# Four graph layers on one core: degree sums two tiles later, the joint share of the row sums added by VectorE, x written by ScalarE, fifth sweep's residual by blocks

## The chip, the cores and the metric

One core of a Trainium2 chip. The metric is the device time of one execution in microseconds; the median of three runs is given, and the profile is of one further execution.

## What is computed

Four graph layers over the same dense 4096 x 4096 matrix `adj` and 4096 x 128 features `x`, each followed by a residual and a layer norm over the 128 features. In short:

```python
# layer 0
inv_deg = 1.0 / (sum(adj, axis=1) + beta)
x = layernorm(x + inv_deg[:, None] * (adj @ x + beta[:, None] * x) @ kernel + bias)
# layer 1
h = x
for W, b in ((W1, b1), (W2, b2), (W3, b3)):       # widths 20, 20, 128
    h = relu(adj @ (h @ W) + b)
x = layernorm(x + relu(h + x))
# layer 2
d = 1.0 / (sqrt(sum(adj, axis=1)) + 1e-8)
x = layernorm(x + d[:, None] * (adj @ (d[:, None] * (x @ W + b))))
# layer 3
S = (x @ W_l) @ (x @ W_r).T
x = layernorm(x + adj @ x + gamma * (softmax(S) @ x) @ W_h @ W_g)
```

## The kernel before

**Stages.** The matrix is read six times (sweeps 0 to 5), then comes the attention part. Sweep 0 is layer 0, sweeps 1 to 3 are the three products of layer 1 (narrow: 20 columns), sweep 4 is layer 2 and sweep 5 is `adj @ x` of layer 3. A sweep has eight rows c (512 nodes each), and a row has 16 half tiles n of 128 x 1024 (512 KB). TensorE accumulates a row in one PSUM bank.

**Split tiles.** A product in full float32 takes TensorE four passes. Where it pays, a tile is split: ScalarE rounds it into t_hi (float32r), VectorE subtracts into t_lo, and TensorE does three single-pass products for each 512 columns, six per tile: t_hi with x_hi and x_lo (L1452, L1453), then t_lo with x_hi (L1456). Both t_hi and t_lo are rings of four, so ScalarE can't start tile u before TensorE has finished tile u-4. In sweep 0 the tiles that are split are, row by row: none; 1, 5, 8, 12, 14, 15; 1, 3, 4, 5, 8, 10, 12, 14, 15; 1, 3, 4, 5, 7, 8, 9, 11, 13, 14, 15; 0, 2, 3, 4, 6 to 11, 13 to 15; all but 4; all; all. The rest are plain (L1460). In sweeps 4 and 5 all tiles are split (L872, L1173, L1607, L1608, L1612).

**Joint tiles.** In sweep 0, tiles whose h is known already are used at once for sweep 1 as well (the joint product, L1469, into another bank, every second tile). With them TensorE also gets their share of the row sums of `adj`, which ScalarE stores in `sums[:, c]` (L749). The tiles that aren't joint (16, 14, 12, 10, 8, 6, 4 and 2 of the rows 0 to 7) are summed by VectorE: `row_sum` into rsum (L986, L990), then `fold` into row_folded (L997).

**The epilogue of a row** runs inside the next row, at places fixed by the tile number n. In sweep 0, for row c-1 inside row c:
- TensorE, after tile 1: `epilogue_1`: e0 (four products with k0, L1349), then e1: for each of four blocks a one-column product of row_folded (L1353) and one of sums with the row picker (L1356; rows 1 to 7 only). After tile 9 the transpose of xn, after tile 11 the product with w1.
- ScalarE: after its tile 2 `evacuate` and `store_ahead`; after tile 4 `second` (square root of the degree sum in e1, L754); after 8 `deviation`; after 10 `normalise` (L774, into xn); after 12 `transposed`.
- VectorE: after tile 4 `residual_1` (degrees, then e0 times inv, L1072), after 5 `residual_2` (plus xb, L1095), after 6 `statistics`, after 8 `scales`; `fold` right after the last tile that isn't joint (tile 15, 13, 13, 13, 13, 11, 7, 1 of the rows 0 to 7).
- GpSimd: xb (L632), then bx (L653), and when xn is there the copy of xn into x (L658).

Each engine works its own list in order, so whatever stands behind a waiting instruction waits too. In sweep 4 the order is alike (all tiles split; `residual_1` L1082 and `residual_2` L1095 at tiles 4 and 5 on VectorE), and GpSimd does stationary5_lo (L639), xb (L635) and the copy into x (L674) for each row. Sweep 5 needs x as st5_hi and st5_lo.

Of the kernel before, what the change touches and what calls it, by code (L numbers as in the profile page):

```python
# [15 lines left out]
P = 128  # L16
# [34 lines left out]
    "xb": (0, 3, 4, 5), "bx": (0,), "xw": (0, 3, 4), "at": range(6), "sq": (0,),  # L51
    "h1": (1, 2), "dinv0": (0,), "deg": (0,), "inv": (0,), "dg2": (0,), "t1": (0, 3, 4),
    "resid": (0, 3, 4), "b3": (3,), "lb": (3,), "bst": (0, 3, 4), "agg": (0, 3, 4), "var": (0, 3, 4), "std": (0, 3, 4),
    "rc": (0, 3, 4), "rstd": (0, 3, 4), "norm": (0, 3, 4), "xt": (0, 3), "ht": (5,), "uw": (0, 1, 2),
    "vw": (3,), "xfin": (5,), "mm1": range(6), "rr": (0,), "mm2": (1, 2), "tx": (0, 3), "mu": (0, 3),
}

# [134 lines left out]
def build(nc, adj_s, x_dram, beta_in, ident_in, comb_in, w, out):  # L192
    with ExitStack() as ctx:
# [46 lines left out]
        with ExitStack() as swp:  # L240
# [26 lines left out]
            xn = sb("xn", [P, CW], F32, swp)  # L267
# [343 lines left out]
        def _(pool):  # L611
# [3 lines left out]
            def keep_old_x(s, c):  # L615

                if s == 5:
                    if first(c):
                        pool.wait_ge(S["resid"], done("resid", 4, NC - 1))
# [3 lines left out]
                    pool.wait_ge(S["xw"], done("xw", 4, NC - 1))  # L623
# [12 lines left out]

            def stationary5_lo(d):
                pool.wait_ge(st5_hi_done, d + 1)
                nc.gpsimd.tensor_tensor(cols(st5_lo, d), cols(x, d), cols(st5_hi, d).bitcast(F32),  # L639
                                        ALU.subtract).then_inc(st5_lo_done, 1)  # L640

            def first_row(c):
                for n in range(NG):
# [11 lines left out]
                    if n == 13 and c > 0:  # L655
                        pool.wait_ge(S["norm"], done("norm", 0, c - 1))
                        alone(pool)
                        nc.gpsimd.tensor_copy(cols(x, c - 1), xn[:, :]).then_inc(S["xw"], 1)  # L658

            def step(s, c, par):  # L660
# [4 lines left out]
                if s == S4 and not (isinstance(c, int) and c < 2):  # L665
                    stationary5_lo(c - 2)
                if s == S5 and first(c):
                    stationary5_lo(NC - 2)
                if ps in STAGES["xb"]:
                    keep_old_x(ps, pc)  # L670
                if ps in STAGES["xw"]:
                    pool.wait_ge(S["norm"], done("norm", ps, pc))
                    alone(pool)
                    nc.gpsimd.tensor_copy(cols(x, row(ps, pc)), xn[:, :]).then_inc(S["xw"], 1)  # L674
                if s == S5 and first(c):
                    stationary5_lo(NC - 1)
# [294 lines left out]
        def _(dve):  # L971
# [785 lines left out]
```

## Time and profile before

| what | us |
|---|---|
| median of 3 runs (1320.33 to 1321.06) | 1320.92 |
| profiled execution | 1323.62 |
| its span, first to last instruction | 1321.8 |
| TensorE busy (share of the span) | 1266.1 (96%) |
| VectorE busy | 969.1 (73%) |
| ScalarE busy | 800.6 (61%) |
| GpSimd busy | 268.5 (20%) |

The rest of the profile is read by stretch: a row of sweep 0 lasts 31 to 39 us, a row of sweeps 4 and 5 22 to 23 us. "Idle before" in a timeline, in square brackets, is how long the engine stood still before that instruction and what ended it. L numbers are lines of the kernel.

### The profile page before, as it was taken

Reading aid. Unit: us, or ns where it says so; the run is one execution under the profiler, and the core shown is the slowest. Engines: PE = TensorE matmul, PEld = TensorE weight load, DVE = VectorE, ACT = ScalarE, POOL = GpSimd, SP = SyncE. Lnnn points to the kernel's source line nnn. Section 1 sums busy time; section 2 is a strip of 40 time slices with the busy share of each in tenths; the row PEclk is TensorE's granted clock in tenths of the full one; section 3 lists DMA queues with packets and bytes.
Section 4 is the critical chain, followed back from the end, with each engine's and each line's share of the span. In section 5 each row is a group of like instructions: output and inputs, shape, how many; then the busy total and the mean of one; then the engine's idle time right before and its main releaser. Section 6 shows DMA issues by size and latency. Waiting matters only on the chain.

```text
span 1321.8 us, 17914 instructions
## 1 busy us (share of the span) xinstructions
PE 1266.1 (96%) x6139; PEld 831.9 (63%) x6139; DVE 969.1 (73%) x1242; ACT 800.6 (61%) x966; POOL 268.5 (20%) x175
## 2 busy tenths in 40 slices
PE   8999999989999899999999999998999999999987
PEld 3566666643332334787877888886676777767764
DVE  7998987620000556999999898877888888778885
ACT  1334556511110224787878777766978787788795
POOL 0211111000000110021112000005333343354355
PEclk9999999889999899999999999999999999999998
DMA  9978766589999699899999999960000000000000
GB/s 366 321 260 311 264 253 248 176 327 346 365 346 409 249 384 383 303 375 356 363 374 345 363 357 386 359 249 0 1 0 0 1 0 1 1 18 14 1 1 32
DMA packets 82817, 294.34 MB, mean 223 GB/s; under 512 B 9658, under 2 KB 11322, under 8 KB 82746
## 3 DMA queue, kind: packets, MB, share of 16 engines
q1 hardware_dynamic: 80496, 292.59, 59.2%
q10 hardware_dynamic: 2250, 0.82, 0.2%
q8 instruction: 43, 0.70, 0.2%
q14 instruction: 28, 0.23, 0.1%
HBM read 291.27 MB, written 2.10 MB: 222 GB/s over the span
## 4 chain that ended last, share of the span: by engine, by line
PE 69%; DVE 12%; ACT 6%; issue 6%; DMA 5%; POOL 1%; DVEq 0%; POOLq 0%; ACTq 0%; SPq 0%
PE acc L1546 8%; PE acc L1612 6%; PE acc L1607 6%; PE acc L1608 6%; PE acc L1694 5%; DMA raw<-in_adj_s 5%; PE acc L1460 4%; PE acc L1452 3%; PE acc L1456 3%; PE acc L1453 3%; DVE peak L1225 3%; DVE t_lo L1173 2%; ACT ring L927 2%; PE rs L1469 2%; PE rs L1551 2%
## 5 line engine op out<-in xcount | busy, mean ns | idle before, releaser
L1173 DVE TENSOR_TENSOR t_lo<-raw,t_hi 128x1024 fp32r<-128x1024 f32 x256 | 311.0, 1259 | 26.6 <-ACT t_hi L872 21.8
L872 ACT ACTIVATE t_hi<-raw 128x1024 fp32r<-128x1024 f32 x256 | 261.6, 1055 | 40.5 <-PE acc L1612 39.5
L1607 PE MATMUL acc<-t_hi,st_hi 128*128 128x512 f32 x512 | 201.9, 394 | 0.8 <-ACT t_hi L872 0.8
L704 POOL TENSOR_TENSOR ring_lo<-ring,p_hi 128x1024 fp32r<-128x1024 f32 x64 | 155.5, 2429 | 219.4 <-ACT p_hi L921 219.3
L1608 PE MATMUL acc<-t_hi,st_lo 128*128 128x512 f32 x512 | 199.5, 390 | 0.0
L1612 PE MATMUL acc<-t_lo,st_hi 128*128 128x512 f32 x512 | 159.5, 393 | 5.8 <-DVE t_lo L1173 5.1
L1247 DVE TENSOR_TENSOR ring<-ring,e 128x1024 f32<-128x1024 f32 x128 | 153.9, 1210 | 0.1
L915 ACT ACTIVATE ring<-ring 128x1024 f32<-128x1024 f32 x128 | 134.2, 1054 | 26.0 <-DVE ring L1247 25.8
L1694 PE MATMUL acc<-ring,x 128*128 128x512 f32 x256 | 120.4, 592 | 0.0
L1612 PEld LDWEIGHTS acc<-t_lo,st_hi 128*128 128x128 f32 x512 | 95.0, 188 | 30.6 <-DVE t_lo L1173 11.4
L1607 PEld LDWEIGHTS acc<-t_hi,st_hi 128*128 128x128 f32 x512 | 96.1, 188 | 21.8 <-DVE st_lo L1033 1.2
L1608 PEld LDWEIGHTS acc<-t_hi,st_lo 128*128 128x128 f32 x512 | 96.2, 188 | 19.8 <-issue 0.2
L1008 DVE TENSOR_TENSOR t_lo<-raw,t_hi 128x1024 fp32r<-128x1024 f32 x72 | 91.4, 1296 | 17.5 <-ACT t_hi L808 17.5
L808 ACT ACTIVATE t_hi<-raw 128x1024 fp32r<-128x1024 f32 x72 | 74.3, 1054 | 37.4 <-PE acc L1456 24.9
L1225 DVE TENSOR_TENSOR peak<-e,peak 128x1024 f32<-128x1024 f32 x54 | 66.1, 1223 | 40.9 <-ACT ring L927 40.8
L1225 DVE TENSOR_TENSOR peak<-rs,peak 128x1024 f32<-128x1024 f32 x61 | 74.5, 1221 | 24.5 <-ACT ring L927 24.0
L674 POOL COPY x<-xn 128x512 f32<-128x512 f32 (+1 forms) x17 | 13.3, 785 | 361.4 <-ACT xn L774 361.4
L1048 DVE TENSOR_TENSOR at<-acc,sums 128x512 f32<-128x512 f32 x19 | 13.1, 689 | 98.8 <-PE acc L1546 84.7
L927 ACT ACTIVATE ring<-rs 128x1024 f32<-128x1024 f32 x62 | 63.3, 1021 | 36.6 <-PE rs L1651 36.1
L1546 PE MATMUL acc<-raw,h_a 128*20 128x512 f32 x384 | 82.7, 601 | 2.5 <-DMA raw<-in_adj_s 1.5
L1460 PE MATMUL acc<-raw,x 128*128 128x512 f32 x160 | 74.6, 610 | 6.5 <-DMA raw<-in_adj_s 6.5
L1452 PE MATMUL acc<-t_hi,x_hi 128*128 128x512 f32 x172 | 77.5, 451 | 0.0
(231 smaller groups left out, 2240.1 us busy)
## 6 DMA issues: line engine op xcount, KB each, us to landing
raw<-in_adj_s SPq DMA_DIRECT2D x518, 512.0 KB, 5.7
kept_t<-in_adj_s SPq DMA_DIRECT2D x8, 512.0 KB, 7.2
x<-in_x SPq DMA_DIRECT2D x4, 512.0 KB, 8.9
kept_l<-in_adj_s SPq DMA_DIRECT2D x4, 512.0 KB, 7.5
kept_s<-in_adj_s SPq DMA_DIRECT2D x4, 512.0 KB, 6.6
kept_v<-in_adj_s SPq DMA_DIRECT2D x4, 512.0 KB, 6.6
kept_e<-in_adj_s SPq DMA_DIRECT2D x4, 512.0 KB, 8.6
kept_late<-in_adj_s SPq DMA_DIRECT2D x4, 512.0 KB, 11.4
```

What stands on the lines that cost most here:

```text
L704: nc.gpsimd.tensor_tensor(ring_lo[:, n % RING, :], slot(n), p_hi[:, m % 2, :].bitcast(F32), ALU.subtract).then_inc(pl_done, 1)
L872: nc.scalar.activation(t_hi[:, g % HL, :], raw[:, k, :], ACT.Copy).then_inc(hi_done, 1)
L915: nc.scalar.activation(slot(n), slot(n), ACT.Exp).then_inc(exped, 1)
L1173: nc.vector.tensor_tensor(t_lo[:, k, :], raw[:, slot_no(s, c, g), :], t_hi[:, k, :].bitcast(F32), ALU.subtract).then_inc(lo_done, 1)
L1225: nc.vector.tensor_tensor(peak[:, :], score_bank(t)[:, :], peak[:, :], ALU.max).then_inc(s_maxed, 1)
L1247: nc.vector.tensor_tensor(part, part, row, ALU.subtract).then_inc(subbed, 1)
L1460: k = mm(a[:, :], block_of(x, b), tile_of(0, c, i)[:, m], start=(n == 0 and m.start == 0), stop=False)
L1546: m = mm(a[k:k + H, :], h_block(s, b), t[:, j * CW:(j + 1) * CW], start=(i.d == items[0].d), stop=(i.d == items[-1].d))
L1607: mm(a[:, :], block_of(st_h, b), hi[:, m], start=(g == 0 and j == 0), stop=False)
L1608: mm(a[:, :], block_of(st_l, b), hi[:, m], start=False, stop=False)
L1612: i = mm(a[:, :], block_of(st_h, b), lo[:, m], start=False, stop=(g == NG - 1 and j == GB - 1))
L1694: r = mm(o, block_of(x, b), slot(n)[:, u * CW:(u + 1) * CW], start=(b == 0), stop=(b == NB - 1))
```

## The change

- Sweep 0, TensorE: `epilogue_1` does e0 alone (S["mm1"]) and doesn't wait for the fold or the stored sums. The four one-column products of row_folded become `degree_sums`, after tile 3, with a semaphore of its own (S["md"]). In the opening of sweep 1 it stands between `fill(0)` and `fill(1)`.
- Sweep 0, VectorE: `whole_sums` at tile 3 multiplies the stored sums by the row picker and adds row_folded, so the four L1356 products go. `fold` is at tile 7 at the earliest. `residual_1` moves from tile 4 to tile 5.
- Sweep 0, ScalarE: `second` keeps its place and waits for S["md"].
- `normalise` writes x; the tile xn, GpSimd's copy and S["xw"] go. xb waits only for the residual sum of the row before.
- Sweep 4, VectorE: `residual_1` is four 128-wide scalar_tensor_tensor (times dinv, plus xb), `residual_2` goes.
- stationary5_lo goes from GpSimd to VectorE (tile 12 of sweep 4's rows from 2 on, tiles 3 and 13 of the first row of sweep 5).

```diff
@@ gpsimd: keep_old_x
                 else:
                     if not (s == 0 and first(c)):
-                        pool.wait_ge(S["resid"], done("resid", s, c) - 1)
-                        pool.wait_ge(S["xw"], done("xw", s, c) - 1)
+                        pool.wait_ge(S[summed(s)], done(summed(s), s, c) - 1)
+                    if s in (3, 4) and first(c):
+                        pool.wait_ge(S["norm"], done("norm", {3: 0, 4: 3}[s], NC - 1))
...
@@ gpsimd: first_row
-                    if n == 13 and c > 0:
-                        pool.wait_ge(S["norm"], done("norm", 0, c - 1))
-                        alone(pool)
-                        nc.gpsimd.tensor_copy(cols(x, c - 1), xn[:, :]).then_inc(S["xw"], 1)
@@ scalar: second
                 if s == 0:
-                    act.wait_ge(S["mm1"], done("mm1", s, c))
+                    act.wait_ge(S["md"], done("md", s, c))
                     nc.scalar.activation(sq[:, :], e1[:, 0:CB], ACT.Sqrt).then_inc(S["sq"], 1)
@@ scalar: normalise
-                    if not (s == 0 and first(c)):
-                        act.wait_ge(S["xw"], done("xw", s, c) - 1)
+                    here = cols(x, row(s, c))
                     for b in range(CB):
-                        i = nc.scalar.activation(block_of(xn, b), block_of(xs, b), ACT.Identity,
+                        i = nc.scalar.activation(block_of(here, b), block_of(xs, b), ACT.Identity,
@@ vector: fold, whole_sums
                 if c > 0:
-                    dve.wait_ge(S["mm1"], done("mm1", 0, c) - 1)
+                    dve.wait_ge(S["md"], done("md", 0, c) - 1)
...
+            def whole_sums(c):
+
+                dve.wait_ge(S["rr"], done("rr", 0, c))
+                if not stored(0, c):
+                    dve.sem_inc(S["rt"], 1)
+                    return
+                dve.wait_ge(sums_done, stored(0, c))
+                nc.vector.scalar_tensor_tensor(out=row_folded, in0=sums[:, c, :], scalar=row_picker,
+                                               in1=row_folded, op0=ALU.mult, op1=ALU.add).then_inc(S["rt"], 1)
@@ vector: first_row
-                    if n == PLAIN[c][-1]:
+                    if n == max(PLAIN[c][-1], 7):
                         fold(c)
                     if c > 0:
-                        if n == 4:
+                        if n == 3:
+                            whole_sums(c - 1)
+                        if n == 5:
                             residual_1(0, c - 1)
-                        if n == 5:
                             residual_2(0, c - 1)
@@ vector: residual_1, sweep 4
-                        nc.vector.tensor_tensor(blocks(xs[:, :]), blocks(e0[:, :]), spread(cols(dinv, c, CB)),
-                                                ALU.mult).then_inc(S["t1"], 1)
+                        dve.wait_ge(S["xb"], done("xb", s, c))
+                        scale = cols(dinv, c, CB)
+                        for b in range(CB):
+                            i = nc.vector.scalar_tensor_tensor(
+                                out=block_of(xs, b), in0=block_of(e0, b), scalar=scale[:, b:b + 1],
+                                in1=block_of(xb, b), op0=ALU.mult, op1=ALU.add)
+                        i.then_inc(S["t1"], 1)
@@ vector: flat, step
+                    whole_sums(pr)
                     residual_1(ps, pr)
...
+                    if s == S4 and g == 12 and not (isinstance(c, int) and c < 2):
+                        stationary5_lo(c - 2)
+                    if s == S5 and first(c) and g in (3, 13):
+                        stationary5_lo(NC - 2 if g == 3 else NC - 1)
@@ tensor: epilogue_1, degree_sums
-                    pe.wait_ge(S["rr"], done("rr", 0, c))
                     for b in range(CB):
-                        mm(e0[:, b * D:(b + 1) * D], block_of(at, b), k0[:, :], start=True, stop=True)
-                    if stored(0, c):
-                        pe.wait_ge(sums_done, stored(0, c))
-                    for b in range(CB):
-                        i = mm(e1[:, b:b + 1], block_of(row_folded, b), ones_f[:, 0:1], start=True,
-                               stop=not stored(0, c))
-                        if stored(0, c):
-                            i = mm(e1[:, b:b + 1], block_of(sums[:, c, :], b), row_picker, start=False, stop=True)
+                        i = mm(e0[:, b * D:(b + 1) * D], block_of(at, b), k0[:, :], start=True, stop=True)
...
+            def degree_sums(c):
+                pe.wait_ge(S["rt"], done("rt", 0, c))
+                for b in range(CB):
+                    i = mm(e1[:, b:b + 1], block_of(row_folded, b), ones_f[:, 0:1], start=True, stop=True)
+                i.then_inc(S["md"], 1)
@@ tensor: first_sweep, opening
                         if n == 1:
                             epilogue_1(0, c - 1, 1 - par)
+                        if n == 3:
+                            degree_sums(c - 1)
...
                     epilogue_1(ps, pr, pr % 2)
                     fill(0)
+                    degree_sums(pr)
                     fill(1)
```

## Rows read from the trace of the kernel before

**Rows 1.** Windows, all engines: stretch, length, busy (count) each, clock, DMA share, GB/s.
```profile
37.00:68.40 31.40, 30.94 (x122) 18.16 (x121) 30.43 (x39) 10.42 (x16) 7.32 (x4) 1.00 0.84 293
...
198.20:232.40 34.20, 34.20 (x192) 23.10 (x190) 25.86 (x36) 20.01 (x26) 4.07 (x3) 1.00 0.68 247
232.40:271.90 39.50, 38.56 (x199) 24.56 (x197) 21.24 (x32) 16.86 (x23) 2.95 (x3) 0.91 0.54 186
...
546.90:569.30 22.40, 22.40 (x102) 18.32 (x101) 21.14 (x30) 18.53 (x23) 2.32 (x3) 1.00 0.98 371
569.30:592.50 23.20, 22.52 (x102) 18.31 (x101) 21.96 (x30) 18.70 (x24) 3.79 (x4) 1.00 0.98 363
```

**Rows 2.** Timeline of TensorE in row 6 of sweep 0: start, length, instruction, count.
```profile
201.04 1.05 PE L1349 MATMUL e<-k,at 128*128 128x128 f32 x8
201.93 0.28 PE L1353 MATMUL e<-ones_f,sums 128*128 128x1 f32 x2
...
203.63 0.49 PE L1452 MATMUL acc<-t_hi,x_hi 128*128 128x512 f32 x1
...
205.12 0.40 PE L1452 MATMUL acc<-t_hi,x_hi 128*128 128x512 f32 x1
...
206.59 0.63 PE L1469 MATMUL rs<-raw,h_a 128*21 128x512 f32 x4
```

**Rows 3.** Groups by line and form, VectorE: busy us, mean ns, idle before.
```profile
L1033 DVE TENSOR_TENSOR st_lo<-v,st_hi 128x512 fp32r<-128x512 f32 x8 | 5.6, 706 | 2.5 <-ACT st_hi L725 2.5
L1079 DVE SCALAR_TENSOR_TENSOR xs<-xs,xb 128x512 f32<-128x512 f32 x8 | 5.5, 692 | 0.3
```

**Rows 4.** Timeline of ScalarE in row 6 of sweep 0.
```profile
199.44 2.01 ACT L808 ACTIVATE t_hi<-raw 128x1024 fp32r<-128x1024 f32 x2
203.81 0.17 ACT L754 ACTIVATE sq<-e 128x4 f32<-128x4 f32 x1 [2.36 <-PE e L1356]
```

**Rows 5.** Timeline of VectorE in row 6 of sweep 0.
```profile
204.11 0.16 DVE L1056 TENSOR_TENSOR deg<-e,beta 128x4 f32<-128x4 f32 x1 [1.22 <-ACT sq L754]
...
205.13 1.22 DVE L1008 TENSOR_TENSOR t_lo<-raw,t_hi 128x1024 fp32r<-128x1024 f32 x1
206.26 0.68 DVE L1095 TENSOR_TENSOR xs<-xs,xb 128x512 f32<-128x512 f32 x1
...
209.13 0.86 DVE L1106 BATCH_NORM_STATS2 stats<-xs 128x6 f32<-128x128 f32 x4
...
211.00 1.22 DVE L1008 TENSOR_TENSOR t_lo<-kept_s,t_hi 128x1024 fp32r<-128x1024 f32 x1
```

**Rows 6.** Timeline of GpSimd in rows 5 and 7 of sweep 0.
```profile
182.91 2.05 POOL L632 TENSOR_TENSOR xb<-x,bias 128x512 f32<-128x512 f32 x1 [0.17 <-POOL x L658]
...
255.03 1.30 POOL L632 TENSOR_TENSOR xb<-x,bias 128x512 f32<-128x512 f32 x1 [0.17 <-POOL x L658]
```

**Rows 7.** Timeline of VectorE in row 5 of sweep 0.
```profile
183.74 2.31 DVE L1008 TENSOR_TENSOR t_lo<-kept_l,t_hi 128x1024 fp32r<-128x1024 f32 x1
```

**Rows 8.** Chain that ended last, in order of time: start, us, what.
```profile
61.93 1.72 PE acc L1460 x4
```

**Rows 9.** Timeline of VectorE in row 7 of sweep 0.
```profile
238.09 0.69 DVE L997 TENSOR_TENSOR sums<-rsum 128x512 f32<-128x512 f32 x1 [7.93 <-PE e L1356]
```

**Rows 10.** Timeline of TensorE in row 7 of sweep 0.
```profile
239.97 1.22 PE L1456 MATMUL acc<-t_lo,x_hi 128*128 128x512 f32 x2 [0.94 <-DVE t_lo L1008]
```

**Rows 11.** Windows of 3 us, TensorE: stretch, length, busy (count), clock, DMA, GB/s.
```profile
240.00:243.00 3.00, 3.00 (x7) 0.50 0.00 0
...
1170.00:1173.00 3.00, 0.30 (x3) 1.00 0.00 0
```

**Rows 12.** Timeline of TensorE in row 2 of sweep 4.
```profile
578.01 0.73 PE L1612 MATMUL acc<-t_lo,st_hi 128*128 128x512 f32 x2 [0.68 <-DVE t_lo L1173]
```

**Rows 13.** Timeline of VectorE in row 2 of sweep 4.
```profile
568.63 3.17 DVE L1173 TENSOR_TENSOR t_lo<-raw,t_hi 128x1024 fp32r<-128x1024 f32 x2 [0.63 <-ACT t_hi L872]
```

**Rows 14.** Timeline of GpSimd in row 2 of sweep 4.
```profile
569.12 1.61 POOL L635 COPY xb<-x 128x512 f32 x1
```

More of the change, by code:

```diff
@@ L50, with summed @@
 STAGES = {
-    "xb": (0, 3, 4, 5), "bx": (0,), "xw": (0, 3, 4), "at": range(6), "sq": (0,),
+    "xb": (0, 3, 4, 5), "bx": (0,), "at": range(6), "sq": (0,),
     "h1": (1, 2), "dinv0": (0,), "deg": (0,), "inv": (0,), "dg2": (0,), "t1": (0, 3, 4),
-    "resid": (0, 3, 4), "b3": (3,), "lb": (3,), "bst": (0, 3, 4), "agg": (0, 3, 4), "var": (0, 3, 4), "std": (0, 3, 4),
+    "resid": (0, 3), "b3": (3,), "lb": (3,), "bst": (0, 3, 4), "agg": (0, 3, 4), "var": (0, 3, 4), "std": (0, 3, 4),
     "rc": (0, 3, 4), "rstd": (0, 3, 4), "norm": (0, 3, 4), "xt": (0, 3), "ht": (5,), "uw": (0, 1, 2),
-    "vw": (3,), "xfin": (5,), "mm1": range(6), "rr": (0,), "mm2": (1, 2), "tx": (0, 3), "mu": (0, 3),
+    "vw": (3,), "xfin": (5,), "mm1": range(6), "rr": (0,), "rt": (0,), "md": (0,), "mm2": (1, 2), "tx": (0, 3), "mu": (0, 3),
 }
+def summed(s):
+    return "t1" if s == 4 else "resid"
 def done(stage, s, r):
@@ L266, in build @@
             xs = sb("xs", [P, CW], F32, swp)
-            xn = sb("xn", [P, CW], F32, swp)
             bx = sb("bx", [P, CW], F32, swp)
@@ L618, in keep_old_x @@
                     if first(c):
-                        pool.wait_ge(S["resid"], done("resid", 4, NC - 1))
+                        pool.wait_ge(S[summed(4)], done(summed(4), 4, NC - 1))
                     else:
@@ L622, in keep_old_x @@
                         pool.wait_ge(S["mm1"], done("mm1", 5, c) - 1)
-                    pool.wait_ge(S["xw"], done("xw", 4, NC - 1))
+                    pool.wait_ge(S["norm"], done("norm", 4, NC - 1))
                 else:
                     if not (s == 0 and first(c)):
-                        pool.wait_ge(S["resid"], done("resid", s, c) - 1)
-                        pool.wait_ge(S["xw"], done("xw", s, c) - 1)
+                        pool.wait_ge(S[summed(s)], done(summed(s), s, c) - 1)
+                    if s in (3, 4) and first(c):
+                        pool.wait_ge(S["norm"], done("norm", {3: 0, 4: 3}[s], NC - 1))
                 alone(pool)
@@ L635, in keep_old_x @@
                     nc.gpsimd.tensor_copy(xb[:, :], cols(x, row(s, c))).then_inc(S["xb"], 1)
[L637 to L640, printed above, removed]
             def first_row(c):
@@ L664, in step @@
                 ps, pc = before(s, c)
[L665 to L668, printed above, removed]
                 if ps in STAGES["xb"]:
                     keep_old_x(ps, pc)
[L671 to L676, printed above, removed]
             chunks(pool, step)
@@ L727, in stationary5_hi @@
             def stationary5_hi(d):
-                act.wait_ge(S["xw"], done("xw", 4, d))
+                act.wait_ge(S["norm"], done("norm", 4, d))
                 nc.scalar.activation(cols(st5_hi, d), cols(x, d), ACT.Copy).then_inc(st5_hi_done, 1)
@@ L1034, in stationary_lo, with stationary5_lo @@
                                         ALU.subtract).then_inc(st_lo_done, 1)
+            def stationary5_lo(d):
+                dve.wait_ge(st5_hi_done, d + 1)
+                nc.vector.tensor_tensor(cols(st5_lo, d), cols(x, d), cols(st5_hi, d).bitcast(F32),
+                                        ALU.subtract).then_inc(st5_lo_done, 1)
             def evacuate_narrow(s, r):
@@ L1063, in residual_1 @@
             def residual_1(s, c):
-                if s in STAGES["resid"]:
+                if s in STAGES["t1"]:
                     dve.wait_ge(S["mm1"], done("mm1", s, c))
@@ L1103, in statistics @@
                 if s in STAGES["bst"]:
-                    dve.wait_ge(S["resid"], done("resid", s, c))
+                    dve.wait_ge(S[summed(s)], done(summed(s), s, c))
                     for b in range(CB):
@@ L1392, in epilogue_3 @@
                     pe.wait_ge(S["norm"], done("norm", s, c))
+                    here = cols(x, row(s, c))
                     for b in range(CB):
-                        i = mm(e2[:, b * D:(b + 1) * D], block_of(xn, b), ident[:, :], is_transpose=True,
+                        i = mm(e2[:, b * D:(b + 1) * D], block_of(here, b), ident[:, :], is_transpose=True,
                                start=True, stop=True)
```

## The prediction

> **What bounds the kernel now.** I read the windows by stage first. In the eight rows of sweep 0, TensorE is busy nearly all the time (30.94 of 31.40 us in row 1, 38.56 of 39.50 in row 7), and in row 1 VectorE is busy as long (30.43) [rows 1]. The DMA share there is 0.54 to 0.84, so loads don't set the pace; both halves of the split (ScalarE's t_hi, VectorE's t_lo) have to stay ahead of TensorE. Sweep 4 is also TensorE's: row 1 takes 22.4 us with no gap, rows 2 to 7 take 23.2 us each with 22.5 us busy [rows 1]. Then I read the timelines of TensorE, ScalarE and VectorE in row 6 of sweep 0, since the change moves work about there, and last the places where TensorE stands still.
>
> **Part 1: joint share off TensorE.** After tile 1 of a row TensorE does e0 (201.04 to 201.93, 0.89 us) and then pairs of one-column products, L1353 and L1356, until 203.63: eight products in 1.70 us, 0.21 each [rows 2]. The change leaves four. Rows 2 to 7 save 6 x 0.85 = 5.1 us of TensorE; row 1 has no joint share. VectorE takes one 512-wide scalar_tensor_tensor (STT) instead; L1079 of that shape takes 0.69 [rows 3], 0.63 in a stream. It comes while VectorE waits for t_hi(3) or t_hi(4), and costs nothing by itself.
>
> **Part 2: the degree sums come two tiles later, and ScalarE waits for them.** This is the term that decides. `second` stays at tile 4 of ScalarE's program but now waits for S["md"], which TensorE gives after tile 3 (I call that moment md; before, the same wait was for the products at tile 1). Behind that wait in ScalarE's queue stand t_hi(5), (6) and on; behind t_hi(5) in VectorE's queue stand t_lo(5), both residuals and the statistics. Before, the square root came at 203.81, with TensorE about to start tile 2 and t_hi up to tile 4 ready (199.44 + 2.01) [rows 4]: a lead of three tiles. VectorE then worked from 204.11 to 211.00 before it could start t_lo(7) [rows 5], and TensorE, which did tiles 2 to 6 meanwhile, didn't catch up with it.
>
> Row 6, step by step, with these durations. TensorE: e0 ends 201.93; tiles 2 and 3 take 1.47 and 1.47 (205.12 to 206.59 is one tile and the switch to the joint product [rows 2]) but 1.36 in a stream: 204.8; the joint product 1.0: 205.8; four sums 0.85: md at 206.7, against 203.7. ScalarE: root, then t_hi(5) at 207.9 (two took 2.01 [rows 4]). VectorE: t_lo(5) 209.0 (1.14, from 205.13 to 206.26 [rows 5]); degrees and first residual 1.02 (204.11 to 205.13): 210.1; second residual 0.60: 210.7; t_lo(6): 211.9; the row sum of tile 6: 1.14; statistics 1.5: (209.13 to 211.00 less a gap of 0.35); t_lo(7) 1.14. Without anything else t_lo(7) is ready at 215.7. GpSimd adds to that. xb(6) used to wait for the copy into x and fell at tiles 12 and 13; now it only waits for the residual before it, so it starts at 210.7, right in VectorE's burst. Such an xb took 1.30 us with VectorE idle and 2.05 with it busy [rows 6], and the t_lo beside it took 2.31 instead of 1.22 [rows 7]. I add 1.3: t_lo(7) at 217.0. TensorE, from 206.7: tile 4 208.1, tile 5 209.6, joint 210.6, tile 6 with a wait of 0.4 212.4, the t_hi part of tile 7 213.3. It waits 3.7 us. Then a row sum, the fold and t_lo(8) make it wait 1.5 again. Row 6: 0.1 + 0.4 + 3.7 + 1.5 - 0.85 = **+4.9 us**.
>
> On the xb step the Trainium skill (SBUF — State Buffer, section SBUF: two separate sides) says that VectorE and GpSimd hold a shared port pair exclusively for a whole instruction, and the loser fully blocks. The 2.31 us agree with that. If the two only shared, the 1.3 would be nearer 0.6.
>
> The same steps in the other rows. Row 1: from md, t_hi(5) 1.2, t_lo(5) 1.2, three row sums 3.4, residuals 1.65, statistics 1.5, t_lo(8) 1.2 make 10.2 us; TensorE reaches that point after 1.72 for each plain tile 4, 6, 7 [rows 8], 1.36 and 1.0: 7.6 us. It waits 2.5, and 0.3 more at the transpose: +2.8. Row 2: waits 1.6, net +0.7. Row 3: 2.4, net +1.5. Row 4 (tile 5 is plain, so VectorE isn't held): 0.4, net -0.5. Row 5: 3.6, net +2.8. Row 7: see part 3. The opening of sweep 1: the sums now stand behind fill(0), 16 records of 1.9 us less the four sums saved, so the chain root, residual, statistics, norm starts 0.9 later: +0.9.
>
> **Part 3: the fold at tile 7.** Only row 7 changes (elsewhere the last plain tile is 7 or later). There the fold at tile 1 waited 7.93 us for TensorE's e1 [rows 9], so t_lo(2) was late and TensorE idle for 0.94 before it [rows 10], 1.1 with the start. After it the granted clock was 0.50 [rows 11], the 1.2 GHz level: products 0.43 apart instead of 0.23 until about 245.5, 2.7 us lost. Both go: -3.8, and -0.85 from part 1. But row 7 gets part 2's waits, with one row sum less: +1.7. Net **-3.0**.
>
> Rows 1 to 7 and opening: 2.8 + 0.7 + 1.5 - 0.5 + 2.8 + 4.9 - 3.0 + 0.9 = +10.1.
>
> **Part 4: x written directly.** ScalarE's norm writes x and GpSimd's copy goes (24 of them). TensorE took xn before, so no chain gets shorter. Nothing waited for the copy but xb and st5_hi. Zero.
>
> **Part 5: sweep 4.** TensorE's stop is one per row, at tile 7 (0.68 us at 578.01 [rows 12], 0.9 with the start). VectorE's way there begins with two t_lo in 3.17 us instead of 2.29, with GpSimd's xb of 1.61 us beside them [rows 13, 14]. Gone: the wait of 0.85 (GpSimd has no st5_lo, and xb no longer falls there), and the second pass of the residual: two 512-wide at 0.60 = 1.2 against four 128-wide. Four 128-wide statistics take 0.86 [rows 5], which is the row nearest, and a 512-wide STT quartered can't be below 0.6; I take 0.83, with bounds 0.6 and 1.2. Added: xb's plain copy now lands in the burst, 0.3 to 0.6. The way gets 0.6 shorter at 0.9 of waiting. st5_lo on VectorE (0.71 alone [rows 3]) stands at tile 12, where VectorE is several tenths ahead each tile (1.14 against 1.36); it costs nothing, but 0.6 a row if that lead is gone. Rows 2 to 7: 6 x 0.7 = **-4.3** (bounds 0 and -5.4). In the first row of sweep 5 a t_lo wait stays about the same: zero.
>
> On four blocks instead of one pass the Trainium skill (VectorE: DVE Perf Modes, Rules for kernel authors) speaks against: the drain comes at every instruction, so keep the count low. The row of four statistics shows 0.2 us each and no more. If each block paid its full lone time instead, the new residual would be no shorter than the old two passes and part 5 would give some 2 us less.
>
> **Part 6: the clock.** After the 3.7 us wait in row 6 it may fall as in row 7. But an interval with only 0.30 of 3 us busy kept 1.00 [rows 11], so length alone doesn't decide. A fall costs 2.7 us less what the next wait hides (0.9). I count one: +1.8; bounds 0 and +8 (rows 1, 5, 6).
>
> **Sum:** +10.1 - 4.3 + 1.8 = +7.6. The profiled execution took 1323.62 us (span 1321.8), 2.7 over the median of 1320.92; in its terms the forecast is 1331.2, in terms of the median **1328.5**.
>
> **Rivals.**
> (A) Faster. The lead holds: TensorE's waits in part 2 don't come, because t_lo(5) to (7) arrive in time. Then -5.1 - 3.8 + 0.9 - 4.3 = -12.3: 1308.6. For it: VectorE is busy only 25.86 us of the 34.20 of row 6 [rows 1]. Against it: three tiles' lead was what hid a burst of 7 us before, and only one tile is left. It decides below a burst of about 3 us. Chance 0.20.
> (B) Slower still, by the clock: it falls in rows 1, 5 and 6, and the blocks cost 1.2 us so that sweep 4 keeps its stop. +10.1 + 5 to 8 - 1: about 1336. For it: 0.94 us of idleness behind one-column products was enough once. Chance 0.15.
> (C) About the same: the waits are two thirds of mine (18 us in all), because xb doesn't fall on VectorE's t_lo and its other steps overlap a little more, and the clock doesn't fall. -6.0 and -1.8 on +7.6: 1320.7. Chance 0.13.
> (D) Forecast, 1324 to 1333: chance 0.52.
>
> Range 1308 to 1335; the likeliest case's own is 1324 to 1333. A measurement of this kernel can tell 0.2% (2.6 us) from no change. Faster by more: A and a part of C, 0.23. Within: most of C, 0.12. Slower: D and B, 0.65.
>
> **What would show it.** Part 1: L1356 has no records in sweep 0 and four products stand behind tile 3. Part 2: TensorE's idle time before t_lo in rows 1, 5 and 6 at tiles 7 and 8, ScalarE's wait before the square root about 5 us instead of 2.4, and rows 5 and 6 longer than 35 us. If ScalarE waits 5 us and TensorE doesn't stop, A is right. Part 3: no VectorE wait before the fold of row 7 and the clock 1.00 there. Part 5: rows 2 to 7 of sweep 4 below 22.7 us. I am wrong if the rows of sweep 0 are shorter than before, or if sweep 4 doesn't shorten.

## The result and the profile after

The changed kernel takes 1328.21 us (median of 5 runs, 1327.15 to 1329.09) against 1320.92 (1319.51 to 1321.82) of the kernel before: ratio 1.0055, interval 1.0041 to 1.007. It is slower by more than 0.2%, 7.3 us where 7.6 had been forecast. The profiled executions took 1328.21 and 1323.62 us, so they show only 4.6 of the 7.3: before's profiled execution stands 2.7 above before's median, after's stands on its own.

All stretches below run from one start of ScalarE's `at` copy to the next, which marks the end of a row on TensorE. A kernel's row is so long:

```
us              row 1   2     3     4     5     6     7   | sweep 4, rows 2 to 7
before          31.47 31.68 32.19 32.65 33.31 34.20 39.33 | 23.2 each
after           35.29 32.84 33.78 32.81 36.23 38.95 36.26 | 22.35 each
difference      +3.8  +1.2  +1.6  +0.2  +2.9  +4.75 -3.1  | -5.15 in all
forecast        +2.8  +0.7  +1.5  -0.5  +2.8  +4.9  -3.0  | -4.3
```

Rows 1 to 7 together are 11.3 us longer. Row 0 adds 0.7 (it differs by as much between kernels whose row 0 is the same), the opening of sweep 1 0.8. Sweep 4 gives back 5.15, and the first row of sweep 5 0.8. That is +6.9. Another 2.5 us of the pair belongs to no edit: the execution before had a fall of TensorE's clock at 438 to 450 us and the one after had none there. That leaves 4.4 of the 4.6 seen; the last 0.2 is spread over the other stretches.

The windows of after, all engines, that answer to [rows 1] (length, then busy and count of TensorE, its weight loads, VectorE, ScalarE and GpSimd, clock, DMA share, GB/s):

```profile
37.88:73.17 35.29, 32.60 (x121) 18.97 (x120) 29.20 (x39) 10.43 (x16) 4.08 (x3) 0.95 0.75 250
172.60:208.83 36.23, 32.91 (x171) 21.71 (x170) 27.78 (x39) 18.54 (x25) 3.15 (x2) 1.00 0.63 232
208.83:247.78 38.95, 35.59 (x181) 22.79 (x180) 27.98 (x38) 19.57 (x26) 3.14 (x2) 0.96 0.60 216
247.78:284.04 36.26, 35.15 (x188) 21.90 (x186) 19.72 (x32) 16.41 (x23) 3.15 (x2) 1.00 0.58 202
...
554.19:576.33 22.14, 22.14 (x101) 18.21 (x100) 21.51 (x32) 18.30 (x23) 2.47 (x1) 1.00 0.98 353
576.33:598.68 22.35, 22.35 (x102) 18.30 (x101) 21.00 (x33) 18.74 (x24) 2.14 (x1) 1.00 1.01 386
```

TensorE was busy in all of row 6 before (34.20 of 34.20); now it is busy 35.59 of 38.95, so 3.36 us are idle, and the rest is work at a lower clock (0.96). In row 7 the clock is back at 1.00 (it was 0.91), and in sweep 4 nothing of the row is idle any more. Row 6 on TensorE, with [rows 2] to compare:

```profile
211.41 1.05 PE L1359 MATMUL e<-k,at 128*128 128x128 f32 x8
...
216.11 1.05 PE L1387 MATMUL e<-ones_f,sums 128*128 128x1 f32 x8
217.03 0.48 PE L1462 MATMUL acc<-t_hi,x_hi 128*128 128x512 f32 x1
...
227.38 1.22 PE L1466 MATMUL acc<-t_lo,x_hi 128*128 128x512 f32 x2 [3.21 <-DVE t_lo L1003]
...
230.38 0.80 PE L1466 MATMUL acc<-t_lo,x_hi 128*128 128x512 f32 x2
```

The sums are four products (eight records, 0.92 us from 216.11 to the next tile), behind the joint product of tile 3. md is at 217.03, 8.2 us after `at` (208.83); by the forecast it was 8.2 us after its `at` too (206.7 against 198.47). Ten microseconds later TensorE stands still 3.21 us before the t_lo part of tile 7. The next two groups say why, ScalarE's and VectorE's timelines:

```profile
217.20 0.17 ACT L740 ACTIVATE sq<-e 128x4 f32<-128x4 f32 x1 [5.39 <-PE e L1387]
217.27 1.06 ACT L793 ACTIVATE t_hi<-raw 128x1024 fp32r<-128x1024 f32 x1
```

```profile
212.04 0.74 DVE L992 SCALAR_TENSOR_TENSOR sums<-sums,comb 128x512 f32<-128x512 f32 x1
...
218.36 1.23 DVE L1003 TENSOR_TENSOR t_lo<-raw,t_hi 128x1024 fp32r<-128x1024 f32 x1 [4.44 <-ACT t_hi L793]
...
219.91 0.69 DVE L1073 TENSOR_TENSOR xs<-e,inv 128x512 f32<-128x512 f32 x1
220.63 0.69 DVE L1101 TENSOR_TENSOR xs<-xs,xb 128x512 f32<-128x512 f32 x1
221.24 1.22 DVE L1003 TENSOR_TENSOR t_lo<-kept_s,t_hi 128x1024 fp32r<-128x1024 f32 x1
222.38 2.30 DVE L975 TENSOR_TENSOR rsum<-rsum,kept_s 128x1024 f32<-128x1024 f32 x1
224.60 0.86 DVE L1112 BATCH_NORM_STATS2 stats<-xs 128x6 f32<-128x128 f32 x4
...
226.11 1.22 DVE L1003 TENSOR_TENSOR t_lo<-kept_s,t_hi 128x1024 fp32r<-128x1024 f32 x1
...
229.11 1.22 DVE L1003 TENSOR_TENSOR t_lo<-raw,t_hi 128x1024 fp32r<-128x1024 f32 x1
```

ScalarE waits 5.39 us for the sums before the root (2.36 before, [rows 4]), with t_hi(5) behind it. VectorE, with the joint share done at 212.7, waits 4.44 us for that t_hi(5), and then has t_lo(5), degrees, two residuals, t_lo(6), a row sum and statistics ahead of t_lo(7), which ends at 227.3. The row sum takes 2.30 us instead of 1.22 because GpSimd's xb runs beside it:

```profile
221.50 2.10 POOL L637 TENSOR_TENSOR xb<-x,bias 128x512 f32<-128x512 f32 x1 [11.48 <-DVE xs L1101]
```

After two of the stops the clock falls. TensorE's windows of 3 us in rows 1 and 6 (busy, count, granted clock):

```profile
54.00:57.00 3.00, 0.67 (x2) 0.91 0.68 206
57.00:60.00 3.00, 3.00 (x6) 0.52 0.80 244
225.00:228.00 3.00, 0.62 (x2) 0.86 1.02 415
228.00:231.00 3.00, 2.93 (x8) 0.57 0.90 363
```

The stops themselves in rows 1 and 5:

```profile
56.33 1.11 PE L1466 MATMUL acc<-t_lo,x_hi 128*128 128x512 f32 x2 [2.69 <-DVE t_lo L1003]
...
187.42 0.73 PE L1466 MATMUL acc<-t_lo,x_hi 128*128 128x512 f32 x2 [2.33 <-DVE t_lo L1003]
190.07 0.74 PE L1466 MATMUL acc<-t_lo,x_hi 128*128 128x512 f32 x2 [0.99 <-DVE t_lo L1003]
```

In all of rows 1 to 7 the timeline marks nine such waits in square brackets, 12.7 us (before: one, 0.94). That isn't their whole price: shorter ones carry no mark, and each stop costs a few tenths more at the start behind it. After the 2.33 us of row 5 the clock stayed at 1.00 (0.73 us for the pair of records, not 1.11).

### The profile page after: what moved, and what is told of

Read it like the earlier page. It is cut to its first block, busy times and chain, and to the rows that moved or that the text cites. A ratio compares the mean times of both kernels' runs of the same rounds, so it can differ in the third digit from the quotient of the medians.

```text
span 1326.4 us, 17780 instructions
## 1 busy us (share of the span) xinstructions
PE 1259.0 (95%) x6083; PEld 824.1 (62%) x6083; DVE 962.1 (73%) x1273; ACT 799.0 (60%) x966; POOL 242.8 (18%) x143
## 4 chain that ended last, share of the span: by engine, by line
PE 72%; DVE 13%; ACT 6%; issue 4%; DMA 3%; POOL 1%; SPq 0%; DVEq 0%; ACTq 0%
PE acc L1625 8%; PE acc L1620 8%; PE acc L1621 8%; PE acc L1559 7%; PE acc L1470 5%; PE acc L1707 4%; DVE peak L1236 3%; DMA raw<-in_adj_s 3%; PE acc L1466 3%; ACT ring L912 2%; PE acc L1462 2%; PE acc L1463 2%; DVE ring L1258 2%; PE rs L1479 2%; PE rs L1564 2%
## 5 line engine op out<-in xcount | busy, mean ns | idle before, releaser
L1180 DVE TENSOR_TENSOR t_lo<-raw,t_hi 128x1024 fp32r<-128x1024 f32 x256 | 303.9, 1230 | 24.1 <-ACT t_hi L857 18.8
L640 POOL COPY xb<-x 128x512 f32<-128x512 f32 (+1 forms) x24 | 32.3, 1347 | 585.1 <-DVE xs L1097 214.2
L1003 DVE TENSOR_TENSOR t_lo<-raw,t_hi 128x1024 fp32r<-128x1024 f32 x72 | 86.2, 1220 | 38.2 <-ACT t_hi L793 38.1
L1559 PE MATMUL acc<-raw,h_a 128*20 128x512 f32 x384 | 79.7, 596 | 3.0 <-DMA raw<-in_adj_s 2.1
```

The lines of the kernel that those rows point to most:

```text
L1180: nc.vector.tensor_tensor(t_lo[:, k, :], raw[:, slot_no(s, c, g), :], t_hi[:, k, :].bitcast(F32), ALU.subtract).then_inc(lo_done, 1)
L1559: m = mm(a[k:k + H, :], h_block(s, b), t[:, j * CW:(j + 1) * CW], start=(i.d == items[0].d), stop=(i.d == items[-1].d))
```

## The experiments

The kernels form three groups, each measured beside the kernel before: 1319.18 us (1316.0 to 1323.61, 23 runs) with ScalarE's wait alone, the fold, the late xb and the two passes; 1320.0 (1316.24 to 1325.67, 17) with the residual behind t_lo, the sums back early, the joint share and the subtraction on GpSimd; 1320.81 (1316.73 to 1324.29, 17) with the opening and the subtraction moved alone. All ratios are to the kernel before of the same group. A single execution differs from another by up to 9 us, and the mean granted clock goes with it: over the 23 runs of the first group the time falls by 1.02 us for each 0.001 of clock (1.32 and 0.79 over the 17 of the other two). So small differences are read from rows of the traces, and the medians stand beside them.

**ScalarE's wait alone moved back.** In after, `second` at ScalarE's tile 6 instead of 4:

```diff
-                    if n == 4:
+                    if n == 6:
                         second(0, c - 1)
```

> The changed kernel, with one move: ScalarE's square root of the degree sum (and with it the wait for the sums) comes after its tile 6 instead of tile 4 in sweep 0. Theory T (the wait in ScalarE's queue holds back t_hi(5) and all that stands behind it): t_hi(5) and (6) are ready before the sums, VectorE's t_lo(5) no longer waits for them, and the TensorE waits of rows 1 to 5 go; row 6 keeps two of about 2 us. Rows 1 to 7 take about 232 to 235 us together instead of 246.2, the whole 1314 to 1318 us. Rival R1 (ScalarE's wait is idle time that costs nothing, and the rows are longer because VectorE has the added joint share and GpSimd's xb in the burst): no change, 1326 to 1330. Rival R2 (the order of the products on TensorE costs it): no change either.

Measured: 1316.08 us (1313.23 to 1318.47), ratio 0.9974 (0.9959 to 0.9988): by the two ratios (1.0055 - 0.9974) some 11 us less than after, and 3 less than before. Rows 1 to 7 are 31.48, 30.85, 31.79, 32.76, 33.11, 37.01, 34.38, sum 231.4 against 246.2. TensorE's marked waits for t_lo fall from 12.7 to 4.5 us, and the clock falls in none of these rows. (The profiled execution, 1313.23 us, was the fastest of the twelve.) So what cost the changed kernel its 11 us was t_hi(5) queued behind ScalarE's wait, not the later sums by themselves. What is left stands in rows 5 and 6 of this kernel on TensorE:

```profile
178.47 0.73 PE L1466 MATMUL acc<-t_lo,x_hi 128*128 128x512 f32 x2 [0.53 <-DVE t_lo L1003]
...
213.87 0.73 PE L1466 MATMUL acc<-t_lo,x_hi 128*128 128x512 f32 x2 [1.92 <-DVE t_lo L1003]
216.86 0.73 PE L1466 MATMUL acc<-t_lo,x_hi 128*128 128x512 f32 x2 [1.34 <-DVE t_lo L1003]
```

**The residual behind t_lo too.** The same, with both residual halves at VectorE's tile 6:

```diff
-                        if n == 5:
+                        if n == 6:
                             residual_1(0, c - 1)
                             residual_2(0, c - 1)
```

> The changed kernel with ScalarE's second wait for the sums moved from tile 4 to tile 6 (as in the run before it) and VectorE's two residual halves both at tile 6. My theory: with the wait at tile 6 ScalarE runs to tile 5 without the row sums, and the remaining waits of TensorE for t_lo come from VectorE, which holds residual_1 and residual_2 ahead of t_lo; at tile 6 these stand behind t_lo of the tile that TensorE wants. Then rows 1 to 7 of the first sweep sum to about 227 us (32.5, 31.5, 31.5, 32.1, 32.3, 33.2, 34.2), 4 less than with the wait alone moved (231.4) and the time is near 1312, 4 less than its 1316. Rival: the residual halves delay nobody once the wait is moved (row 5 and 6 are long because TensorE's clock falls in them): the sum stays at 231 and the time at 1316. Rival on the other side: residual_2 a tile later delays the next row's first reader of the residual: rows grow by up to 1 us each, time near 1320.

Measured: 1310.97 us (1308.17 to 1313.13), ratio 0.9923 (0.9899 to 0.9947). Rows 31.5, 30.8, 31.2, 31.8, 32.35, 34.0, 34.4, sum 226.0 (227 expected). TensorE's work in these rows is that of after, and the clock stays at 1.00, so the 20.2 us between the two sums (246.2 and 226.0) are the price of the waits and falls that after has and this kernel hasn't. In row 6 one short wait is left:

```profile
211.73 0.72 PE L1466 MATMUL acc<-t_lo,x_hi 128*128 128x512 f32 x2 [0.51 <-DVE t_lo L1003]
```

**The sums back early, ScalarE untouched.** The other way to the same end:

```diff
                         if n == 1:
                             epilogue_1(0, c - 1, 1 - par)
-                        if n == 3:
                             degree_sums(c - 1)
...
-                        if n == 3:
+                        if n == 2:
                             whole_sums(c - 1)
```

(and residual_1 at 4, residual_2 at 5, as before the change)

> The changed kernel with the degree sums' products back on TensorE right after e0, as early as in the kernel before, VectorE's whole_sums at its tile 2, residual_1 at 4, residual_2 at 5; ScalarE's wait stays at tile 4, the joint share stays on VectorE. If the delay of the sums is what cost the changed kernel its 11 us in rows 1 to 7, undoing it alone gives it back and keeps the gain of the share: rows 1 to 7 sum to about 228 us, time near 1312 to 1314. Rival: what costs is VectorE's own added work (the share, t_lo of the fifth sweep) and not the place of the sums: the rows stay near 246 and the time near 1328. Rival: TensorE now waits at tile 1 for VectorE's share: about 1 us in each of seven rows, time near 1320.

Measured: 1311.28 us (1308.64 to 1312.48), ratio 0.9929 (0.9905 to 0.9952); rows 1 to 7 sum to 226.3. The joint share is ready on VectorE in time for sums at tile 1. Both cures give the same rows, so the place of the sums and the place of the wait are one fault seen from two sides: the wait must not come ahead of its products.

**The joint share alone put back.** The kernel with wait and residual at tile 6, with the four products of the joint share on TensorE again. VectorE's instruction for them goes (`whole_sums` only passes its semaphore on); of the rest of the edit this is the part on TensorE:

```diff
-                    i = mm(e1[:, b:b + 1], block_of(row_folded, b), ones_f[:, 0:1], start=True, stop=True)
+                    i = mm(e1[:, b:b + 1], block_of(row_folded, b), ones_f[:, 0:1], start=True,
+                           stop=not stored(0, c))
+                    if stored(0, c):
+                        i = mm(e1[:, b:b + 1], block_of(sums[:, c, :], b), row_picker, start=False, stop=True)
```

> The kernel of the first run of this call with the joint share put back on TensorE (four more one-column products in the degree sums of each row from row 1 on) and off VectorE. It prices the edit by itself: 0.85 us a row in seven rows by my sum, so 5 to 6 us slower than that first run, about 1317 to 1318. Rival: the four products lie in time in which TensorE waits anyway: no change, 1312. Rival: the share on VectorE holds t_lo back: with it gone the kernel is 1 to 3 us faster, 1310.

Measured: 1314.64 us (1310.81 to 1322.03, 12 runs), 3.7 above its partner of the same group. Rows 1 to 7: 31.6, 31.7, 32.5, 32.3, 33.2, 34.6, 35.3, sum 231.2 against 226.0: 5.2 us, where part 1 had 5.1. The term was right.

**The fold alone.** In before, one line:

```diff
-                    if n == PLAIN[c][-1]:
+                    if n == max(PLAIN[c][-1], 7):
                         fold(c)
```

> The kernel before, with the fold at tile 7 at the earliest and nothing else (only row 7 of sweep 0 changes). T: VectorE's wait of 7.93 us in row 7 goes, TensorE's stop of 0.94 us at tile 2 goes, and the granted clock stays at 1.00 there: row 7 from 39.3 to about 35.5 us, the whole 3.8 us faster, 1317. Rival: the fall of the clock comes from the sixteen one-column products ahead of it and stays: 1 us faster at most, 1320.

Measured: row 7 is 35.39 us against 39.33, as expected, but the median is 1318.7 (1314.64 to 1321.22), ratio 0.9992 (0.9978 to 1.0005): not told apart from no change, and not the 1317 expected. (The products ahead of the stop are eight; sixteen is the count of their records.) The row of before's profile isn't found in every execution, as the run of the subtraction moved alone shows further down.

**xb out of the burst.** In after, GpSimd's xb in sweep 0 waits for the norm of the row before:

```diff
+                    if s == 0 and not first(c):
+                        pool.wait_ge(S["norm"], done("norm", 0, c) - 1)
```

> The changed kernel, with xb in sweep 0 waiting for the norm of the row before, so that it falls at tiles 11 to 13 as it did before. T (an xb in VectorE's burst costs it a whole instruction): row 6 of sweep 0 from 38.95 to about 37.7 us, rows 1, 3, 5 and 7 the same within 0.3, rows 2 and 4 longer by 0.7 and 1.3 because xb falls on a t_lo that TensorE needs there; the whole about the same, 1327 to 1330. Rival (GpSimd and VectorE only share the port): all rows within 0.4.

Measured: 1332.29 us (1329.93 to 1334.53), ratio 1.0092 (1.0066 to 1.0118). Row 6 is 1.1 us shorter (37.83), rows 2 and 4 are 1.1 and 1.0 longer (33.94, 33.85). xb beside VectorE costs 1.1 us where it falls, and moving it only moves the place. Row 5 is 0.4 longer (36.66), which wasn't expected. TensorE in rows 5 and 6 of this kernel:

```profile
189.67 1.15 PE L1468 MATMUL acc<-t_lo,x_hi 128*128 128x512 f32 x2 [2.33 <-DVE t_lo L1005]
...
228.98 0.73 PE L1468 MATMUL acc<-t_lo,x_hi 128*128 128x512 f32 x2 [2.13 <-DVE t_lo L1005]
...
231.97 0.73 PE L1468 MATMUL acc<-t_lo,x_hi 128*128 128x512 f32 x2 [1.34 <-DVE t_lo L1005]
```

In row 5 the clock falls behind the same 2.33 us that had no fall in after; that is the 0.4. In row 6 the first stop is 1.08 us shorter than after's 3.21, no fall follows, and a second stop of 1.34 us stands where after had the fall. From the start of the first t_lo part to the start of the product behind the second it is 3.57 us here and 3.64 in after (227.38 to 231.02). So the fall in after's row 6 cost 0.1 us and no more: t_lo(8) was ready only at 230.33 (229.11 + 1.22), whatever TensorE's clock.

The median missed the expected 1327 to 1330: it is 4 us above after's. Its clock was lower (0.988 in the mean against 0.991), which is most of that, and whether the late xb causes the additional falls is open.

**Sweep 4, one part at a time.** Three kernels. First, after with the residual of sweep 4 in two passes again:

```diff
-                        for b in range(CB):
-                            i = nc.vector.scalar_tensor_tensor(
-                                out=block_of(xs, b), in0=block_of(e0, b), scalar=scale[:, b:b + 1],
-                                in1=block_of(xb, b), op0=ALU.mult, op1=ALU.add)
+                        nc.vector.tensor_tensor(blocks(xs[:, :]), blocks(e0[:, :]), spread(cols(dinv, c, CB)),
+                                                ALU.mult).then_inc(S["t1"], 1)
```

> The changed kernel, with sweep 4's residual in two passes of 512 columns again (times dinv, then plus xb a tile later). T (my sum for sweep 4: most of the gain is GpSimd's work out of the way of the first two t_lo, and the four blocks save 0.4 us of 1.2): rows 2 to 7 of sweep 4 from 22.36 to 22.5 to 22.8 us, the whole 1 to 2.5 us slower, 1329 to 1331. Rival (the blocks are the whole gain): rows back at 23.2, the whole 5 us slower, 1333. Rival (the blocks cost as much as the passes, each paying its full time): no change.

Measured: rows 2 to 7 take 22.6 us each (22.35 after): 1.5 us in sweep 4. The median of 1334.08 (1329.09 to 1335.6), ratio 1.0099 (1.0071 to 1.0127), is 6 above after's, beyond the 1329 to 1331 expected; three of its four runs had a clock of 0.985 or 0.986, the fourth had 0.992 and took 1329.09. The trace's 1.5 is the price of the passes; the rest goes with the clock, and why it fell more often isn't settled.

Sweep 0 of this kernel is that of after, instruction for instruction, and so is the stop in row 1. But no fall follows it here (0.74 us for the pair, not 1.11):

```profile
55.37 0.74 PE L1461 MATMUL acc<-t_lo,x_hi 128*128 128x512 f32 x2 [2.68 <-DVE t_lo L1003]
```

The row takes 34.48 us where after took 35.29: the fall of row 1 cost 0.8 us.

Second, after with the subtraction st5_lo back on GpSimd:

```diff
+            def stationary5_lo(d):
+                pool.wait_ge(st5_hi_done, d + 1)
+                nc.gpsimd.tensor_tensor(cols(st5_lo, d), cols(x, d), cols(st5_hi, d).bitcast(F32),
+                                        ALU.subtract).then_inc(st5_lo_done, 1)
```

> The changed kernel with the remainder of the stationary operand in the fifth sweep (a subtraction of one block) put back from VectorE onto GpSimd, as before the change. In the changed kernel the rows of that sweep fell from 23.2 to 22.35 us. If moving this subtraction gave that (GpSimd no longer stands in the way of VectorE's copies, or no longer delivers it late), rows 2 to 7 go back to about 23.0 us and the time grows by 3 to 4 us, to about 1332. Rival: the residual by blocks alone gave the gain: rows stay at 22.4, time stays near 1328. Rival: part and part, rows at 22.7, time near 1330.

Measured: 1334.29 us (1333.59 to 1335.59), ratio 1.0105 (1.008 to 1.0131); rows 2 to 7 take 23.11 us. Nearly the whole gain of the sweep is gone although the residual is still by blocks. GpSimd's and VectorE's timelines at the turn of a row of it show the burst of [rows 13, 14] again:

```profile
647.92 1.37 POOL L644 TENSOR_TENSOR st_lo<-x,st_hi  x1 [20.19 <-ACT st_hi L726]
649.24 1.61 POOL L640 COPY xb<-x 128x512 f32 x1
```

```profile
648.73 3.20 DVE L1191 TENSOR_TENSOR t_lo<-raw,t_hi 128x1024 fp32r<-128x1024 f32 x2 [0.59 <-ACT t_hi L868]
651.85 1.11 DVE L1097 SCALAR_TENSOR_TENSOR xs<-e,dinv,xb 128x128 f32<-128x128 f32 x4
```

Two t_lo take 3.20 us beside GpSimd's two operations. In after, where only xb is there, it is GpSimd that is slowed and the two t_lo take 2.35. The same copy took 2.49 us there and 0.62 in the first row of the sweep, where VectorE has nothing to do:

```profile
543.11 0.62 POOL L640 COPY xb<-x 128x512 f32<-128x512 f32 x1 [29.04 <-ACT x L759]
...
649.14 2.49 POOL L640 COPY xb<-x 128x512 f32 x1 [19.86 <-DVE xs L1086]
```

```profile
647.76 1.12 DVE L1086 SCALAR_TENSOR_TENSOR xs<-e,dinv,xb 128x128 f32<-128x128 f32 x4
648.80 2.35 DVE L1180 TENSOR_TENSOR t_lo<-raw,t_hi 128x1024 fp32r<-128x1024 f32 x2
```

Third, before with the subtraction alone moved to VectorE's tile 12 (the four lines of `stationary5_lo` and its calls, as in the change):

```diff
+                    if s == S4 and g == 12 and not (isinstance(c, int) and c < 2):
+                        stationary5_lo(c - 2)
```

> The kernel before with one edit alone: the subtraction that makes the remainder of the stationary operand in the fifth sweep moved from GpSimd to VectorE at its tile 12; residual still in two passes, x still copied by GpSimd. Theory: GpSimd's subtraction and its copy of x stand beside VectorE's first two t_lo and stretch them from 2.35 to 3.2 us, and that makes TensorE's stop of about 0.7 us a row; with the subtraction away rows 2 to 7 of the fifth sweep go from 23.2 to about 22.6 us, as in the changed kernel with the residual in two passes, and the time is 4 us less, about 1316. Rival: the copy of x alone keeps the stop, and it took the direct writing of x as well: rows stay at 23.1, time 1320.

Measured: 1317.14 us (1313.11 to 1320.78), ratio 0.9972 (0.9958 to 0.9986); rows 2 to 7 take 22.86 us, between theory (22.6) and rival (23.1). Together: 23.2, the subtraction moved 22.86, x also written directly 22.6, blocks too 22.35; without the subtraction moved, the other two give only 0.1 of it (23.11). That the direct x is worth the middle 0.25 is read from two kernels of different bases and wasn't tried alone.

This run also holds row 7 of sweep 0 with the old fold: VectorE's wait of 7.93 us and TensorE's stop are just those of [rows 9, 10], and the clock doesn't fall behind them:

```profile
238.27 0.69 DVE L986 TENSOR_TENSOR sums<-rsum 128x512 f32<-128x512 f32 x1 [7.93 <-PE e L1354]
```

```profile
240.15 0.73 PE L1454 MATMUL acc<-t_lo,x_hi 128*128 128x512 f32 x2 [0.94 <-DVE t_lo L997]
```

```profile
240.00:243.00 3.00, 2.85 (x16) 1.00 0.00 0
```

The row takes 36.58 us. Of the 39.33 in before's profile, 2.75 are the clock of that one execution; the fold itself is worth 1.2 (36.58 to 35.39). That fits a median that its run alone moved so little. Of two profiled executions one has the fall; how often it comes isn't known.

**The opening.** Two kernels, those of the two cures, with the last degree sums ahead of the first fill:

```diff
                     epilogue_1(ps, pr, pr % 2)
-                    fill(0)
                     degree_sums(pr)
+                    fill(0)
                     fill(1)
```

> The kernel with ScalarE's second wait and both residual halves at tile 6 and the last degree sums ahead of the first fill. Theory: 0.8 us less than the same kernel with the sums behind the fill (1311.0), near 1310. Rival: no change, 1311.

> The changed kernel with the degree sums' products right after e0 in every row, the last one in the opening of the second sweep too (there they stood behind the first fill). That last place is all that is new beside the run with the sums at tile 1. My sum put the opening at 0.9 us, and the offset of the changed kernel kept 0.8 us there. Theory: 0.8 us less than that run, about 1310.5. Rival: the opening waits for the last VectorE share instead, and TensorE's fill stands behind it: no gain or up to 1 us slower, 1311 to 1312.

Measured: 1305.91 us (1304.78 to 1309.06), ratio 0.9884 (0.9868 to 0.99), and 1306.45 (1304.98 to 1308.12), ratio 0.9882 (0.9865 to 0.9899). Both are about 5 us less than without the edit. The traces show a smaller gain: from `at` to the first xt of sweep 1 it is 18.11 us against 19.21 in the first pair and 18.00 against 20.47 in the second, and at the end of sweep 4 the kernels are 1.65 and 3.2 us ahead of their partners. In the second pair part of it is a shorter fall of the clock. TensorE's wait for x in the opening, first without and then with the edit (first pair):

```profile
274.34 1.12 PE L1404 MATMUL e<-ident,x 128*128 128x128 f32 x4 [4.36 <-ACT x L759]
```

```profile
272.71 0.66 PE L1404 MATMUL e<-ident,x 128*128 128x128 f32 x4 [2.64 <-ACT x L759]
```

Clock explains part of the other 3.4 of the first pair: the runs with the edit had 0.993 in the mean, those without 0.991, some 2 us by the slope above. In the profiled execution without the edit the clock also falls at 909, 1158 and 1263 us, in the one with it nowhere between 438 and 1296, and these places lie far behind the edit. Whether the shorter wait is the reason for the higher clock isn't settled; the kernels were also in different groups. Either way, these two are faster than before by 1.2%, and than after by some 22 us.

## Why the prediction was right, and where it wasn't

The mechanism is shown: the wait for the sums at ScalarE's tile 4 holds back t_hi(5), VectorE's burst comes late, and TensorE stands before t_lo. Moving the wait alone gives back 15 us of rows. The number came out too (1328.5 against 1328.21), but that it did to 0.3 us is luck. The sum went from one profiled execution to another: +7.6, to 1331.2. That execution took 1328.21: the edits made +6.9, and 2.5 went with before's fall at 438 us, which has nothing to do with them. Then 2.7 was taken off as before's distance from its median, as if after's profile stood as far above its own; it stood on it. The terms:

- **Part 1** (joint share, 6 x 0.85): right, 5.2 in rows when it is put back alone.
- **Part 2**, md at 206.7: right to a tenth; the wait before the root 5.4 us, as said. Of the 20.2 us of rows that the kernel with wait and residual at tile 6 saves, 0.9 are the two falls, so the waits cost 19.3 where my steps had some 18. Only the marks in the timeline add up to less, 12.7. In row 6 I had 0.4, 3.7 and 1.5; the marked one is 3.21. The third, before t_lo(8), was hidden by the fall; where the clock stayed up it was there, at 1.34 (the run with the late xb). So rival C's "two thirds of mine" fits the marks and not the rows. xb fell on the row sum, not on t_lo(7), at 1.1 instead of 1.3. One reading was wrong: [rows 6] has no xb "with VectorE idle". Beside the xb at 255.03 two t_lo that start at 255.07 took 3.47 us instead of 2.35; xb came first and took its 1.30, and VectorE paid. The Trainium skill (SBUF — State Buffer, section SBUF: two separate sides) has the shared port pair as an exclusive lock. The trace agrees: xb starts at 221.50 behind a t_lo that has begun and takes 2.10; the row sum starts at 222.38 and ends 1.08 later than it would alone, and xb ends at 223.60. The pair in sweep 4, where xb is slowed and t_lo isn't, shows that the loser can be either.
- **Part 6**, the clock: one fall was counted, at 1.8; there were two in these rows, after the stops of 2.69 and 3.21 us, and they cost 0.8 and 0.1, the second because t_lo(8) came no sooner. The row sums were forecast at 9.2 + 1.8 and came to 11.3: 1.3 more of waits, 0.9 less of clock.
- **Part 3**, the fold at tile 7: its step took the fall at 240 us as part of every execution. It is in before's profiled one and not in that of the kernel with the subtraction moved alone, with the very same wait. In terms of the profile -3.0 was right (-3.1); in terms of the median the gain is up to 2.75 us smaller, by how often the fall comes. The fold put in alone moved the median by 0.5 us, where 3.8 had been expected. This is the step that failed, and the subtraction of one uniform 2.7 us from the sum hid it.
- **Part 4**: the opening and the rows show no cost of the direct x; in sweep 4 it may have its share of the gain.
- **Part 5**: -5.15 and -0.8 for -4.3 (6 x 0.7 is 4.2) and 0. The stop is gone altogether. The reasons were in the wrong proportion: the blocks take 1.12 us (1.04 to the next start, 0.26 each) where I took 0.83, near my upper bound, and are worth 0.25 us a row. The larger share comes from GpSimd's two operations, which no longer stretch the two t_lo; I had named that 3.17 us and given it no price beyond the wait, and xb in the burst, put at 0.3 to 0.6, cost VectorE nothing. The Trainium skill (VectorE: DVE Perf Modes, Rules for kernel authors) says to keep the number of instructions low. The trace agrees in part: four blocks came out 0.2 us dearer than I had them, and still below the two passes.
- **Opening**: +0.8 for +0.9. Put ahead of the fill it gives back 1.1 and 2.5 in the two pairs of traces, the second with a shorter fall of the clock in it.

Rival A needed the lead to hold. It shows what the change could have been: with the wait and the residual in the right place it is 1311, and 1306 with the opening, on either side of A's 1308.6.

## What to carry to other kernels

When products are moved later on one engine, look at every engine whose program waits for them and move the wait by as many tiles, together with what stands behind it; the cost isn't the wait but the work of the next tiles queued behind it. Price the stops that follow by the length of the stretch with and without them, not by the marks in a timeline (12.7 us of marks, 19.3 of rows here). Take a fall of the clock out of a profiled execution before you price the stop that it follows: look in a second execution whether the same stop draws it. And when a small operation is moved off an engine, price first what it did to its neighbour, then what it took itself.

## What the runs showed of the hardware

- The same stop doesn't always draw a fall of the clock. 0.94 us behind the same products had a granted clock of 0.50 after it in one execution and 1.00 in another. Four profiled executions have the stops of after's row 1 and row 5: behind 2.69 us (2.68 in one) the clock fell in three of them, behind 2.33 us in one. Behind 3.21 to 3.23 us it fell in all three that have that stop.
- What a fall costs depends on what waits behind it: 2.75 us in row 7 of before, 0.8 in row 1, 0.4 in row 5, 0.1 in row 6, where VectorE's t_lo(8) came no sooner. With the two passes row 6 had the same stop and a longer fall and took 1.4 more (40.35 against 38.95).
- The mean granted clock of executions of the kernel before ranged from 0.987 to 0.995, and the time by up to 9 us with it, about 1.02 us for each 0.001 (0.79 to 1.32 by group).
- VectorE's row sum beside GpSimd's xb took 2.30 us instead of 1.22; two t_lo beside two GpSimd operations 3.20 instead of 2.35; beside one, 2.35, with GpSimd's copy at 2.49 instead of 0.62. So either engine can be the one that waits.
